# A graph-attention kernel's first stretch: index conversion moved to ScalarE, loads reordered, two blocks of work exchanged

## The chip, the cores and the metric

The kernel runs on one core of one Trainium2 chip. The metric is the device time of one execution in microseconds (us). Three runs of the kernel before gave 1695.93, 1697.75 and 1699.25 us; their median is 1697.75 us.

## The reference

The kernel computes one graph-attention layer with a residual and a layer norm. There are 6250 nodes of 96 features (4 heads of 24), and 200000 edges, each with a source and a destination node, sorted by destination.

```
q = (x[src] @ qW).reshape(e, 4, 24)
k = (x[dst] @ kW).reshape(e, 4, 24)
v = (x[dst] @ vW).reshape(e, 4, 24)
exp_s = exp(clip(einsum('ehd,ehd->eh', q, k), -10, 10))
norms = segment_sum(exp_s, src)[src]
w = exp_s / (norms + 1e-8)
res = segment_sum(w[:, :, None] * v, src).reshape(6250, 96)
out = layernorm(x + (x + res))
```

Here the edges' sources (`src`) are what the sums run over, and they are in no order; the destinations (`dst`) are sorted.

## The kernel before, in words

The program has four stretches: a first stretch that projects the nodes and makes all index tables (0 to about 133 us), a first phase that sorts the edges by source tile (`first_phase`, L434), a second phase that attends over the sorted edges (`second_phase`, L450), and the layer norm with the stores. The change touches the first stretch alone.

Each engine has its own program, and all its instructions run in the order in which they are written there; semaphores tie the engines together. In the first stretch two kinds of work are interleaved by hand.

**Projection of the nodes.** The 6250 nodes are 12 tiles of 512 nodes (`TI` = 12, t = 0 to 11) and a rest. For tile t, SyncE (SP) loads the rows (`rows_of_x`, L720) into a ring of three buffers. TensorE turns them (`turn_x`, L982, into one_c or one_d), ScalarE copies the turned tile to SBUF (`turned_x`, L843), and TensorE multiplies by the three weights (`project`, L991, one half into two_a and one into two_b). Then the float32 result is cut into three bfloat16 parts: `high` on ScalarE (L851), `rest_of` on VectorE (L1235: the projection less its high part), `mid` on ScalarE (L860), the low part on GpSimd (POOL, L607), and `keep_q` on ScalarE (L864). GpSimd also clears a tenth of `acc` (L611) behind each of the first ten. SP writes the parts to the table in HBM (L750) and issues four transfers that clear rows (`clear`, L713) in every step t. `project(t)` overwrites two_a and two_b, so it waits for `rest_of(t - 1)`.

**Index tables.** The source and destination of every edge are loaded as int32 in two arrays of 112 rows by 1792 (`edge_i`, `dest_i`; L726, L733, L736: three transfers each, 672, 105 and 4 KB). VectorE converts both to float32 (`edge_f`, L1249; `dest_f`, L1251). TensorE turns the sources in four groups (`sources`, L1008, into meta and sum_bank), VectorE copies each group out as int32 (L1274), and four VectorE instructions of 1568 elements split the node numbers into tile and place (L1277 to L1280, called the four bit operations below). The destinations follow in the steps t = 2 and 3 (`targets`, L1015, copied out by ScalarE at L880). From t = 4 on, seven pieces of a histogram are made (VectorE L1326, TensorE L1038, VectorE L1334), then prefix sums.

**Constants.** GpSimd fills its constant tiles at the start (L545 to L602). VectorE waits for them (`consts`) and derives twelve small constants from them (L1257 to L1269).

The order on the engines around the change: PE does `turn_x(0)`, waits for the weights, and then in every step `turn_x(t + 1)`, `project(t)`; `sources()` stands behind `project(1)`. ScalarE does `turned_x(0)`, `turned_x(1)`, and then per step `mid(t - 1)`, `keep_q(t - 2)`, `high(t)`, `turned_x(t + 2)`. VectorE does the conversion of the sources, `rest_of(0)`, the conversion of the destinations, `rest_of(1)`, the constants, the four copies of turned sources, the four bit operations, `rest_of(2)`, and then the destinations' part. SP issues x tile 0, both first pieces of the edges, the three weights, the four smaller pieces of the edges, x tiles 1 and 2, and then goes on by steps.

Of the kernel before, what the change touches and what calls it, by code (L numbers as in the profile page):

```python
# [16 lines left out]
ALU = mybir.AluOpType  # L17
ACT = mybir.ActivationFunctionType
# [13 lines left out]
COLS = 14  # L32
# [21 lines left out]
HI, LO = 7, 8  # L54
# [7 lines left out]
def gnn_program(nc, x, src, dst, wq, wk, wv, out):  # L62
# [57 lines left out]
    with ExitStack() as ctx:  # L120
# [3 lines left out]
        def sem(name):  # L124
            return ctx.enter_context(nc.semaphore(name))
# [209 lines left out]
        consts = sem("consts")  # L335
        later_consts = sem("later_consts")
        loads = sem("loads")
        edges_in = sem("edges_in")
        dve_step = sem("dve_step")
        edges_f = sem("edges_f")  # L340
        turned_src = sem("turned_src")
# [180 lines left out]
        def columns_of(held, n):  # L522
            return held[:, :, 4 * n:4 * n + turn_cols(n)].rearrange("p i k -> p k i")

        def turned_edges(n):
            return turn_in[n % 2][:, 0:turn_cols(n) * ITERS].rearrange("p (k i) -> p k i", k=turn_cols(n))
# [185 lines left out]
        def _(sp):  # L712
# [7 lines left out]
            def rows_of_x(t):  # L720
                sp.dma_start(x_in[:, t % XRING], x[t * TSLOT * P:(t + 1) * TSLOT * P, :].rearrange("(s p) d -> p s d", p=P)
                             ).then_inc(x_loaded[t % XRING], 16)

            rows_of_x(0)
            for flat, held in ((src, edge_i), (dst, dest_i)):
                sp.dma_start(held[0:EDGE_ROWS, :], flat[0:EDGE_ROWS * EIT].rearrange("(i e) -> i e", e=EIT)  # L726
                             ).then_inc(edges_in, 16)
            for n, w in enumerate((wk, wv, wq)):
                sp.dma_start(weights[0:D, n * D:(n + 1) * D], w).then_inc(loads, 16)

            sp.wait_ge(dve_step, 2)
            for flat, held in ((src, edge_i), (dst, dest_i)):
                sp.dma_start(held[EDGE_ROWS:ITERS - 1, :],  # L733
                             flat[EDGE_ROWS * EIT:(ITERS - 1) * EIT].rearrange("(i e) -> i e", e=EIT)
                             ).then_inc(edges_in, 16)
                sp.dma_start(held[ITERS - 1:ITERS, 0:EREST],  # L736
                             flat[(ITERS - 1) * EIT:E].rearrange("(i e) -> i e", i=1)).then_inc(edges_in, 16)
            for t in range(1, XRING):
                rows_of_x(t)
            for t in range(TI):  # L740
                if t + XRING <= TI:
# [100 lines left out]
        def _(act):  # L842
# [21 lines left out]
            def keep_q(t):  # L864
                act.wait_ge(low_made, t + 1)
                act.activation(q3[:, t * TSLOT:(t + 1) * TSLOT], parts3[:, t % 2, :, 2], ACT.Copy).then_inc(q_kept, 1)

            turned_x(0)
            turned_x(1)
            for t in range(TI + 1):  # L870
                if t >= 1:
                    mid(t - 1)
                if t >= 2:
                    keep_q(t - 2)
                if t < TI:
                    high(t)
                for n in TARGETS_AT.get(t, ()):

                    act.wait_ge(turned_dst, n + 1)
                    act.activation(columns_of(dcol_i, n), turned_edges(n), ACT.Copy).then_inc(kept_dst, 1)  # L880
                if t + 2 <= TI:
                    turned_x(t + 2)
# [95 lines left out]
        def _(pe):  # L978
# [91 lines left out]
            turn_x(0)  # L1070
            pe.wait_ge(loads, 48)
            for t in range(TI):
                turn_x(t + 1)
                project(t)
                if t == 1:
                    sources()
                if t in TARGETS_AT:
                    targets(TARGETS_AT[t])
                if t == BASES_AT:
                    bases()  # L1080
                for i in PIECES_AT.get(t, ()):
                    if i == 0:
                        pe.wait_ge(consts, NCONST)
                    piece(i)
                if t == 8:
                    totals()
                if t == 9:
                    starts()
                if t == 10:
                    steps()  # L1090
                if t == 11:
                    tiles_of_blocks()
# [131 lines left out]
        def _(dve):  # L1224
# [20 lines left out]
                                                last3[0:NREST, :, 0], ALU.subtract)  # L1245
                    ins.then_inc(rest_made, 1)

            dve.wait_ge(edges_in, 96)
            dve.tensor_copy(edge_f[0:ITERS], edge_i[0:ITERS]).then_inc(edges_f, 1)  # L1249
            rest_of(0)  # L1250
            dve.tensor_copy(dest_f[0:ITERS], dest_i[0:ITERS]).then_inc(edges_f, 1)  # L1251
            rest_of(1)

            dve.wait_ge(consts, NCONST)
            last = slice(P - 32, P)
# [11 lines left out]
            link(dve.tensor_scalar(tail_col, place_i[:, 1:2], float(P), float(P * FULL), ALU.mult, ALU.add))  # L1267
            link(dve.tensor_scalar(select_h, spread_h, next_col, None, ALU.is_equal))
            link(dve.scalar_tensor_tensor(select_h, spread_h, high_col, select_h, ALU.is_equal, ALU.subtract))  # L1269


            for n in range(4):
                dve.wait_ge(turned_src, n + 1)
                dve.tensor_copy(columns_of(col_i, n), turned_edges(n)).then_inc(kept_src, 1)  # L1274
            dve.wait_ge(kept_src, 4)
            bits = edge_i.rearrange("p (g c) -> p g c", c=COLS)[:, 0:NG]
            link(dve.tensor_scalar(bits, col_i, 7, LO - 1, ALU.logical_shift_right, ALU.bitwise_and))  # L1277
            link(dve.tensor_copy(src_lo, bits))
            link(dve.tensor_single_scalar(bits, col_i, 7, ALU.logical_shift_right))
            link(dve.tensor_copy(src_tile, bits))  # L1280
            rest_of(2)


# [370 lines left out]
```

## Time and profile before

| what | value |
|---|---|
| median of three runs | 1697.75 us |
| the profiled execution's own time | 1694.7 us |
| span of its trace | 1692.6 us |
| granted TensorE clock, mean over the span | 0.933 |
| PE busy | 1471.8 us (87%) |
| DVE busy | 1468.6 us (87%) |
| ACT busy | 1013.3 us (60%) |
| POOL busy | 1016.2 us (60%) |

PE is TensorE, PEld its weight loads, DVE VectorE, ACT ScalarE, POOL GpSimd, SP SyncE. The profile follows one execution. The own time is the span and about 2 us around it. The shares of busy time are means over four stretches that have different limits, so for a change in the first 133 us the stretch has to be looked at by itself. The granted clock is given as a share of 2.4 GHz: 1.00 is 2.4 GHz, 0.50 is 1.2 GHz.

### The profile page before, as it was taken

What the parts mean: (1) busy time and instruction counts of PE and PEld (TensorE: products, weight loads), DVE (VectorE), ACT (ScalarE), POOL (GpSimd) and SP (SyncE); (2) the same over time, 40 slices, a digit from 0 to 9 for tenths busy, and PEclk for the clock granted to TensorE, in tenths of its full rate; (3) what the DMA queues carried; (4) which work ended last, traced back from release to release, by engine and by line L of the source; (5) the groups of instructions that cost most, each with busy time, mean ns of one, the idle gap of its engine ahead of it and who ended that gap; (6) DMA issues with size and microseconds to landing.
All of it is one profiled execution on the core that took longest, in us unless ns stands there. A gap on an engine that the chain in (4) does not pass through costs nothing.

```text
span 1692.6 us, 56067 instructions
## 1 busy us (share of the span) xinstructions
PE 1471.8 (87%) x19964; PEld 1414.8 (84%) x19965; DVE 1468.6 (87%) x2980; ACT 1013.3 (60%) x1844; POOL 1016.2 (60%) x764
## 2 busy tenths in 40 slices
PE   4873988899888888898759999999999999999990
PEld 3652888888888888788759999999999999999990
DVE  6988999898898989989148999999999999999987
ACT  3341666566665666666536666666666666666654
POOL 6230777777777777767625555555555555555551
PEclk7565999999999999999979999999999999999995
DMA  5673899999999999999887777777777777777732
GB/s 166 225 273 132 310 373 357 351 334 360 345 364 344 352 351 350 367 318 371 328 297 258 243 242 241 244 246 246 241 244 241 243 245 246 244 241 241 244 113 57
DMA packets 159451, 465.03 MB, mean 275 GB/s; under 512 B 36994, under 2 KB 59266, under 8 KB 152244
## 3 DMA queue, kind: packets, MB, share of 16 engines
q1 hardware_dynamic: 123572, 301.16, 54.5%
q0 software_dynamic: 35840, 163.36, 24.1%
q8 instruction: 23, 0.38, 0.1%
q14 instruction: 16, 0.13, 0.0%
HBM read 271.21 MB, written 209.73 MB: 284 GB/s over the span
## 4 chain that ended last, share of the span: by engine, by line
PE 79%; DVE 9%; issue 7%; SPq 2%; DMA 2%; ACT 1%; POOL 0%; DVEq 0%; POOLq 0%; ACTq 0%
PE two_a L1133 14%; PE meta L1195 13%; PE sum_bank L1195 12%; PE two_b L1133 12%; PE two_a L1216 7%; PE two_b L1216 7%; PE one_c L1206 3%; PE one_d L1206 3%; PE meta L1151 2%; PE one_d L1162 2%; PE sum_bank L1115 1%; SPq L826 1%; DMA work<-kv_table 1%; DVE work L1472 1%; DVE acc L1618 1%
## 5 line engine op out<-in xcount | busy, mean ns | idle before, releaser
L699 POOL TENSOR_TENSOR work<-work 128x768 f32<-128x768 f32 x236 | 452.3, 1917 | 346.4 <-ACT work L941 346.4
L636 POOL DMA_INDIRECT sorted_rows<-work x448 | 501.1, 1118 | 209.6 <-issue 209.0
L1133 PE MATMUL two_a<-work 128*128 128x192 bf16 x2688 | 269.8, 252 | 80.1 <-issue 78.7
L1133 PEld LDWEIGHTS two_a<-work 128*128 128x128 f16 x2688 | 221.1, 100 | 100.8 <-issue 82.4
L904 ACT ACTIVATE work<-two_a 128x768 f32<-128x768 f32 x224 | 181.8, 811 | 179.8 <-PE two_a L1133 179.5
L1133 PE MATMUL two_b<-work 128*128 128x192 bf16 x2688 | 267.1, 251 | 0.0
L950 ACT ACTIVATE work<-work 128x1024 f32<-128x1024 bf16 x236 | 247.5, 1049 | 0.0
L1195 PE MATMUL meta<-work 128*128 128x100 f32 x1888 | 236.9, 279 | 0.9 <-DVE acc L1550 0.9
L1195 PE MATMUL sum_bank<-work 128*128 128x100 f32 x1888 | 235.2, 278 | 0.0
L1583 DVE TENSOR_REDUCE work<-work 128x32 f32<-128x768 f32 x236 | 224.9, 953 | 8.2
L1133 PEld LDWEIGHTS two_b<-work 128*128 128x128 f16 x2688 | 225.5, 100 | 6.7
L1195 PEld LDWEIGHTS meta<-work 128*128 128x128 f32 x1888 | 221.8, 193 | 1.0 <-issue 1.0
L1195 PEld LDWEIGHTS sum_bank<-work 128*128 128x128 f32 x1888 | 220.1, 192 | 0.0
L904 ACT ACTIVATE work<-two_b 128x768 f32<-128x768 f32 x224 | 181.9, 812 | 48.6 <-PE two_b L1133 48.2
L941 ACT ACTIVATE work<-work 128x32 f32<-128x32 f32 x236 | 54.1, 229 | 257.5 <-DVE work L1558 257.5
L1566 DVE TENSOR_TENSOR work<-work,node_row 128x1024 bf16<-128x1024 bf16 x236 | 161.9, 686 | 25.6 <-ACT work L934 25.6
L1216 PE MATMUL two_a<-q,work 128*128 x2832 | 141.9, 207 | 4.6 <-ACT work L947 4.6
L1216 PE MATMUL two_b<-q,work 128*128 x2832 | 140.4, 206 | 0.0
L1216 PEld LDWEIGHTS two_a<-q,work 128*128 128x128 bf16 x2832 | 130.3, 99 | 5.4 <-issue 5.2
L1574 DVE TENSOR_TENSOR work<-two_a,work 128x768 f32<-128x768 f32 x118 | 113.0, 958 | 23.6 <-PE two_a L1216 16.5
L1574 DVE TENSOR_TENSOR work<-two_b,work 128x768 f32<-128x768 f32 x118 | 113.0, 958 | 22.1 <-PE two_b L1216 22.0
L1216 PEld LDWEIGHTS two_b<-q,work 128*128 128x128 bf16 x2832 | 129.3, 98 | 0.0
(229 smaller groups left out, 2205.8 us busy)
## 6 DMA issues: line engine op xcount, KB each, us to landing
work<-sorted_rows SPq DMA_DIRECT2D x472, 392.0 KB, 3.5
work<-sorted_local SPq DMA_DIRECT2D x56, 1024.0 KB
sorted_rows<-pad_rows SPq DMA_DIRECT2D x49, 392.0 KB, 4.5
work<-kv_table SPq DMA_DIRECT2D x112, 144.0 KB
sorted_rows<-work POOLq DMA_INDIRECT x448
kv_table<-work SPq DMA_DIRECT2D x12, 576.0 KB, 3.4
work<-in_x SPq DMA_DIRECT2D x12, 192.0 KB, 3.8
sorted_local<-work SPq DMA_DIRECT2D x56, 8.0 KB
```

What stands on the lines that cost most here:

```text
L636: pool.indirect_dma_start(out=rows_dram, out_offset=bass.IndirectOffsetOnAxis(ap=place_now[:, p, u, b:b + 1], axis=0), in_=payload[:, p, u ...
L699: pool.tensor_tensor(now[:, :, 0:D].rearrange("p c (h f) -> p c h f", h=HEADS), blk[:, k, :, :, D:2 * D].rearrange("p m c (h f) -> p (m c) ...
L904: act.activation(payload[:, p, u, KPART * part:KPART * (part + 1), 0:2 * D].rearrange("p (b k) w -> p b k w", b=2), kv_ps[part % 2], ACT.C ...
L941: act.activation(msg[:, k % MSGS, :, D:AW], clipped[:, k], ACT.Exp).then_inc(exp_made[k % PSEM], 1)
L950: act.activation(hot_f[:, k % HOTF], hot[:, k % HOTS], ACT.Copy).then_inc(hotf_made[k % PSEM], 1)
L1133: mm = pe.matmul(to, picked[:, u % 2, k * P:(k + 1) * P], window[:, u, :, n, :], start=(n == 0), stop=(n == 2))
L1195: mm = pe.matmul(sums[k % 2][:, m, :], hot_f[:, k % HOTF, m * BLK + c, :], msg[:, k % MSGS, m * BLK + c, :], start=(c == 0), stop=(c == BL ...
L1206: mm = pe.transpose(turned[k % 2][:, c, :], hot[:, k % HOTS, c, :], ident_b[:])
L1216: mm = pe.matmul(q_ps[k % 2][:, m, c, :], hot_T[:, k % 2, m * BLK + c, :], q3[:, bass.ds(tile, 1), i, :].rearrange("p a d -> p (a d)"), st ...
L1566: dve.tensor_tensor(hot[:, k % HOTS].rearrange("p c (n i) -> p c n i", i=TWIN), tags[:, k].unsqueeze(2).to_broadcast([P, CH, P // TWIN, TW ...
L1574: dve.tensor_tensor(qk.rearrange("p (m c) d -> p m c d", m=PAIR), q_ps[k % 2], blk[:, k, :, :, 0:D], ALU.mult).then_inc(qk_made[k % PSEM], 1)
L1583: dve.tensor_reduce(score[:, k], qk.rearrange("p c (h f) -> p (c h) f", h=HEADS), AX.X, ALU.add).then_inc(score_made[k % PSEM], 1)
```

## The change

ScalarE converts both index arrays, through a new function `floats`, instead of VectorE. The semaphore `edges_in`, which counted all six transfers of the edges (96), is split into `sources_in` and `targets_in` (48 each). SP issues x tile 0, the weights, the sources, x tile 1, the destinations, x tile 2. TensorE does `project(0)` ahead of `turn_x(1)`. ScalarE does `high(0)`, the sources' conversion, `turned_x(1)`, the destinations' conversion, and goes on as before. On VectorE the copies of the turned sources and the four bit operations stand ahead of the constants.

```diff
-        edges_in = sem("edges_in")
+        sources_in = sem("sources_in")
+        targets_in = sem("targets_in")
...
+            def edges(flat, held, done):
+
+                sp.dma_start(held[EDGE_ROWS:ITERS - 1, :],
+                             flat[EDGE_ROWS * EIT:(ITERS - 1) * EIT].rearrange("(i e) -> i e", e=EIT)
+                             ).then_inc(done, 16)
+                sp.dma_start(held[ITERS - 1:ITERS, 0:EREST],
+                             flat[(ITERS - 1) * EIT:E].rearrange("(i e) -> i e", i=1)).then_inc(done, 16)
+
             rows_of_x(0)
-            for flat, held in ((src, edge_i), (dst, dest_i)):
-                sp.dma_start(held[0:EDGE_ROWS, :], flat[0:EDGE_ROWS * EIT].rearrange("(i e) -> i e", e=EIT)
-                             ).then_inc(edges_in, 16)
             for n, w in enumerate((wk, wv, wq)):
                 sp.dma_start(weights[0:D, n * D:(n + 1) * D], w).then_inc(loads, 16)
-
+            sp.dma_start(edge_i[0:EDGE_ROWS, :], src[0:EDGE_ROWS * EIT].rearrange("(i e) -> i e", e=EIT)
+                         ).then_inc(sources_in, 16)
             sp.wait_ge(dve_step, 2)
...
-            for t in range(1, XRING):
+            edges(src, edge_i, sources_in)
+            rows_of_x(1)
+            sp.dma_start(dest_i[0:EDGE_ROWS, :], dst[0:EDGE_ROWS * EIT].rearrange("(i e) -> i e", e=EIT)
+                         ).then_inc(targets_in, 16)
+            edges(dst, dest_i, targets_in)
+            for t in range(2, XRING):
                 rows_of_x(t)
...
+            def floats(held, ints, done):
+                act.wait_ge(done, 48)
+                act.activation(held[0:ITERS], ints[0:ITERS], ACT.Copy).then_inc(edges_f, 1)
+
             turned_x(0)
-            turned_x(1)
             for t in range(TI + 1):
...
                 if t < TI:
                     high(t)
+                if t == 0:
+                    act.wait_ge(dve_step, 2)
+                    floats(edge_f, edge_i, sources_in)
+                    turned_x(1)
+                    floats(dest_f, dest_i, targets_in)
...
             for t in range(TI):
-                turn_x(t + 1)
-                project(t)
+                if t == 0:
+                    project(t)
+                    turn_x(t + 1)
+                else:
+                    turn_x(t + 1)
+                    project(t)
...
-            dve.wait_ge(edges_in, 96)
-            dve.tensor_copy(edge_f[0:ITERS], edge_i[0:ITERS]).then_inc(edges_f, 1)
             rest_of(0)
-            dve.tensor_copy(dest_f[0:ITERS], dest_i[0:ITERS]).then_inc(edges_f, 1)
             rest_of(1)
+
+            for n in range(4):
+                dve.wait_ge(turned_src, n + 1)
+                dve.tensor_copy(columns_of(col_i, n), turned_edges(n)).then_inc(kept_src, 1)
...
             dve.wait_ge(consts, NCONST)
```

The instructions on ScalarE from its start, before the change (one_c and one_d hold a turned tile, two_a and two_b the halves of a projection):

```order
L849 ACTIVATE work<-one_c 96x512
L849 ACTIVATE work<-one_d 96x512
L857 ACTIVATE work<-two_a 128x6x96
L857 ACTIVATE work<-two_b 128x6x96
L849 ACTIVATE work<-one_c 96x512
L862 ACTIVATE work<-work 128x12x96
L857 ACTIVATE work<-two_a 128x6x96
L857 ACTIVATE work<-two_b 128x6x96
```

and with it:

```order
L855 ACTIVATE work<-one_c 96x512
L863 ACTIVATE work<-two_a 128x6x96
L863 ACTIVATE work<-two_b 128x6x96
L876 ACTIVATE work<-work 112x1792
L855 ACTIVATE work<-one_d 96x512
L876 ACTIVATE work<-work 112x1792
L855 ACTIVATE work<-one_c 96x512
L868 ACTIVATE work<-work 128x12x96
L863 ACTIVATE work<-two_a 128x6x96
L863 ACTIVATE work<-two_b 128x6x96
```

The two conversions (L876) stand ahead of everything that ScalarE does for tile 1 and later, the second of them behind the copy of turned tile 1.

VectorE from `rest_of(1)` to `rest_of(2)`, before the change (of the twelve constants the first and the last ones are shown, in two pieces):

```order
L1242 TENSOR_TENSOR work<-two_b,work 128x576
L1257 TENSOR_SCALAR work<-work 32x512
L1258 SCALAR_TENSOR_TENSOR work<-work 32x512
```

```order
L1268 TENSOR_SCALAR work<-work 128x1024
L1269 SCALAR_TENSOR_TENSOR work<-work 128x1024
L1274 CAST work<-meta 128x4x112
L1274 CAST work<-sum_bank 128x4x112
L1274 CAST work<-meta 128x4x112
L1274 CAST work<-sum_bank 128x2x112
L1277 TENSOR_SCALAR work<-work 128x1568
L1278 CAST work<-work 128x1568
L1279 TENSOR_SCALAR work<-work 128x1568
L1280 CAST cols_work<-work 128x1568
L1242 TENSOR_TENSOR work<-two_a,work 128x576
```

and with it:

```order
L1260 TENSOR_TENSOR work<-two_b,work 128x576
L1271 CAST work<-meta 128x4x112
L1271 CAST work<-sum_bank 128x4x112
L1271 CAST work<-meta 128x4x112
L1271 CAST work<-sum_bank 128x2x112
L1274 TENSOR_SCALAR work<-work 128x1568
L1275 CAST work<-work 128x1568
L1276 TENSOR_SCALAR work<-work 128x1568
L1277 CAST cols_work<-work 128x1568
L1282 TENSOR_SCALAR work<-work 32x512
L1283 SCALAR_TENSOR_TENSOR work<-work 32x512
```

The copies (L1271) and the bit operations (L1274 to L1277) now follow `rest_of(1)` at once, and the constants stand between them and `rest_of(2)`.

## Rows read from the trace of the kernel before

**Rows 1.** The page: share of the chain that ended last, by engine
```profile
PE 79%; DVE 9%; issue 7%; SPq 2%; DMA 2%; ACT 1%; POOL 0%; DVEq 0%; POOLq 0%; ACTq 0%
```

**Rows 2.** Windows: stretch, busy us of PE, PEld, DVE, ACT, POOL, clock, DMA, GB/s
```profile
0.00:12.20 12.20, 1.06 (x4) 0.65 (x5) 1.31 (x3) 1.88 (x2) 11.56 (x34) 1.00 0.92 187
12.20:21.00 8.80, 5.38 (x16) 3.86 (x16) 8.78 (x2) 2.37 (x4) 8.80 (x19) 1.00 0.60 208
21.00:70.50 49.50, 32.93 (x116) 25.23 (x117) 45.58 (x53) 21.07 (x27) 14.86 (x14) 0.60 0.55 197
70.50:101.00 30.50, 30.50 (x118) 27.00 (x118) 22.17 (x30) 11.36 (x15) 7.67 (x5) 0.58 0.65 229
101.00:132.90 31.90, 15.17 (x41) 8.62 (x38) 28.11 (x57) 14.81 (x19) 11.56 (x8) 0.58 0.77 285
```

**Rows 3.** Chain of waits in order of time: start us, us, what
```profile
5.31 6.81 DMA work<-in_dst
...
12.22 8.78 DVE work L1249
...
132.92 1.33 DVE work L1412
```

**Rows 4.** Timeline, 0 to 28 us: start us, us, engine, line, operation, [idle <-releaser]
```profile
4.48 0.59 ACT L849 ACTIVATE work<-one_c 96x512 f32<-96x512 f32 x1 [2.40 <-PE one_c L988]
...
5.60 1.49 SPq L721 DMA_DIRECT2D work<-in_x  x3
...
12.79 1.06 PE L988 MATMUL one_d<-ident_f,work 128*96 128x128 f32 x4 [8.35 <-DMA work<-in_x]
...
13.64 2.13 PE L997 MATMUL two_a<-work 96*128 96x288 f32 x4
...
17.73 0.65 ACT L857 ACTIVATE work<-two_b 128x576 bf16<-128x576 f32 x1 [1.27 <-PE two_b L997]
...
21.15 0.10 POOL L602 MEMSET start_i<- 1x9 int32 x1
...
21.80 2.26 PE L997 MATMUL two_a<-work 96*128 96x288 f32 x4 [3.62 <-DVE work L1242]
22.24 1.08 DVE L1251 CAST work<-work 112x1792 f32<-112x1792 int32 x1
...
25.77 0.95 PE L1004 MATMUL meta<-ident_f,work 112*128 112x112 f32 x4
...
26.69 0.76 DVE L1242 TENSOR_TENSOR work<-two_b,work 128x576 f32<-128x576 f32 x1 [1.16 <-ACT work L857]
```

**Rows 5.** Timeline, 27 to 43 us
```profile
27.48 0.35 DVE L1257 TENSOR_SCALAR work<-work 32x512 bf16<-32x512 bf16 x1
...
32.14 0.92 DVE L1274 CAST work<-meta 128x448 int32<-128x448 f32 x1
...
35.51 0.98 DVE L1277 TENSOR_SCALAR work<-work 128x1568 int32<-128x1568 int32 x1
...
37.14 2.59 POOL L607 TENSOR_TENSOR work<-work 128x1152 bf16<-128x1152 f32 x1 [10.72 <-ACT work L862]
37.53 3.48 DVE L1279 TENSOR_SCALAR work<-work 128x1568 int32<-128x1568 int32 x1
...
39.67 0.52 POOL L611 MEMSET acc<- 128x500 f32 x1
...
42.06 0.76 DVE L1242 TENSOR_TENSOR work<-two_a,work 128x576 f32<-128x576 f32 x1
```

**Rows 6.** Groups of ScalarE by form, 0 to 140 us: busy us, mean ns
```profile
L862 ACT ACTIVATE work<-work 128x1152 bf16<-128x1152 f32 x12 | 13.9, 1157 | 11.9 <-DVE work L1242 11.9
...
L880 ACT ACTIVATE work<-meta 128x448 int32<-128x448 f32 x2 | 1.9, 944 | 0.0
```

**Rows 7.** By line, one instruction's ns min/median/max: the projection; a histogram piece
```profile
L997 PE MATMUL two_b<-work x48: 406/684/687, 15.6 to 124.2; 96*128 96x288 f32 x48
...
L1038 PE MATMUL meta<-work x42: 409/413/419, 60.4 to 88.2; 128*112 128x128 f16 x42
```

More of the change, by code:

```diff
@@ L722, in rows_of_x @@
                              ).then_inc(x_loaded[t % XRING], 16)
+            def edges(flat, held, done):
[4 more added lines that the diff above has]
+                             flat[(ITERS - 1) * EIT:E].rearrange("(i e) -> i e", i=1)).then_inc(done, 16)
             rows_of_x(0)
-            for flat, held in ((src, edge_i), (dst, dest_i)):
-                sp.dma_start(held[0:EDGE_ROWS, :], flat[0:EDGE_ROWS * EIT].rearrange("(i e) -> i e", e=EIT)
-                             ).then_inc(edges_in, 16)
             for n, w in enumerate((wk, wv, wq)):
                 sp.dma_start(weights[0:D, n * D:(n + 1) * D], w).then_inc(loads, 16)
+            sp.dma_start(edge_i[0:EDGE_ROWS, :], src[0:EDGE_ROWS * EIT].rearrange("(i e) -> i e", e=EIT)
+                         ).then_inc(sources_in, 16)
             sp.wait_ge(dve_step, 2)
[L732 to L737, printed above, removed]
-            for t in range(1, XRING):
+            edges(src, edge_i, sources_in)
[4 more added lines that the diff above has]
+            for t in range(2, XRING):
                 rows_of_x(t)
@@ L1246, in rest_of @@
                     ins.then_inc(rest_made, 1)
-            dve.wait_ge(edges_in, 96)
-            dve.tensor_copy(edge_f[0:ITERS], edge_i[0:ITERS]).then_inc(edges_f, 1)
             rest_of(0)
-            dve.tensor_copy(dest_f[0:ITERS], dest_i[0:ITERS]).then_inc(edges_f, 1)
             rest_of(1)
+            for n in range(4):
+                dve.wait_ge(turned_src, n + 1)
+                dve.tensor_copy(columns_of(col_i, n), turned_edges(n)).then_inc(kept_src, 1)
+            dve.wait_ge(kept_src, 4)
+            bits = edge_i.rearrange("p (g c) -> p g c", c=COLS)[:, 0:NG]
+            link(dve.tensor_scalar(bits, col_i, 7, LO - 1, ALU.logical_shift_right, ALU.bitwise_and))
+            link(dve.tensor_copy(src_lo, bits))
+            link(dve.tensor_single_scalar(bits, col_i, 7, ALU.logical_shift_right))
+            link(dve.tensor_copy(src_tile, bits))
             dve.wait_ge(consts, NCONST)
@@ L1269, in _ @@
             link(dve.scalar_tensor_tensor(select_h, spread_h, high_col, select_h, ALU.is_equal, ALU.subtract))
[L1272 to L1280, printed above, removed]
             rest_of(2)
```

## The prediction

> **What bounds the kernel now.** The page's split of the chain that ended last says PE 79% and VectorE 9% [rows 1], but that is a mean over the whole span. The change ends where the first phase begins, at 132.92 us [rows 3], so I read the first stretch alone. The windows come first [rows 2]. From 0 to 12.2 us VectorE does 1.31 us of work, then it is full: 8.78 of 8.80 us, then 45.58 of 49.50 us. From 70.5 to 101 us TensorE is full (30.50 of 30.50), and after that VectorE again (28.11 of 31.90). The chain in order of time says what stands at the start [rows 3]: a transfer of the destinations that lands at 12.12, and behind it one instruction of VectorE, the conversion of the sources (L1249), 8.78 us long.
>
> The timeline shows why that is odd [rows 4]. The same instruction on the destinations (L1251, same shape) takes 1.08 us at 22.24. The long one begins at 12.22 and ends at 21.00; GpSimd is busy for 8.80 of the 8.80 us from 12.2 to 21.0 [rows 2], and its last constant ends at 21.25 [rows 4]. So 7.7 of the 8.78 us are VectorE waiting for GpSimd. Everything hangs behind it: `rest_of(0)`, and TensorE's `project(1)`, which starts at 21.80 after 3.62 us idle, released by VectorE.
>
> **The change part by part.**
>
> *Project 0 ahead of turn 1.* ScalarE has turned tile 0 at 5.07 [rows 4]. Before, `project(0)` starts at 13.64, behind x tile 1 (TensorE idle 8.35 us on that transfer). Now it needs only the weights. Their landing is not shown; they follow x tile 0 directly, so at least 5.1, and at most 3.0 + 6.8 = 9.8 us (they are issued by about 3.0, at 0.5 us per issue as the three of 1.49 us at 5.60 [rows 4], and the slowest transfer shown took 6.81 us, behind a full queue [rows 3]). I take 5.4, near the lower end, since x tile 0 alone is ahead. From its start, `high(0)` ends 4.74 us later (18.38 - 13.64), so at 10.1, and `rest_of(0)`, two instructions of 0.75, ends at about 10.9. VectorE then is free for ten microseconds in which it was waiting.
>
> *Loads.* Before, x tile 1 was issued from 5.60 and TensorE started on it at 12.79 [rows 4]. In the new order the same bytes stand ahead of x tile 2 as did before: all edges, the weights, tiles 0 and 1. Tile 2 is 192 KB behind tile 1; at the 208 to 229 GB/s of the windows [rows 2] that is 0.8 to 0.9 us, so tile 2 lands at about 13.5. The destinations land between 12.1 and 12.8, plus what x tile 1 ahead of them adds: about 13.0. The sources land earlier, at about 8: they and what is ahead of them are 1.1 MB of the 1.9 MB that had landed at 12.12, counted from 2. If the queue were no faster for them they land at 12.1; then ScalarE's two conversions run back to back from 12.1 to 15.5, which costs about 0.5.
>
> *Conversion on ScalarE.* No row shows it. Nearest below: 1152 elements in 1157 ns (L862), which for 1792 gives 1.8 us. Nearest above: ScalarE writing int32, 448 elements in 944 ns (L880) [rows 6], 2.1 ns each, 3.8 us. L880 reads PSUM and writes with a stride; L862 goes from SBUF to SBUF in rows like the conversion, so I take 1.8. ScalarE then has: sources' conversion 10.1 to 11.9; `turned_x(1)` (0.59) to 12.5; destinations' conversion 13.0 to 14.8; `turned_x(2)` to 15.4; `mid(0)` (1.16) to 16.6.
>
> *Tile 1.* TensorE turns tile 2 at 13.5 (0.85 to the projection, as 12.79 to 13.64), and `project(1)` starts at 14.35, against 21.80: 7.45 us earlier. `high(1)` needs its first half at 16.6; ScalarE is free at 16.6. That is tight, but nothing is lost. `rest_of(1)` ends 5.65 us after the start of `project(1)` (27.45 - 21.80), so at 20.0. `sources()` begins 3.97 us after `project(1)` (25.77 - 21.80) and the first group is turned at about 19.3, so VectorE goes from `rest_of(1)` straight to the copies.
>
> *Sources ahead of constants.* Moving the constants costs and saves VectorE nothing by itself: 27.48 to 32.11, 4.6 us [rows 5], only stand elsewhere. TensorE and ScalarE get the sources 4.6 us earlier, but `project(3)` waits for `rest_of(2)`, which still stands behind both blocks. What the move changes is which of VectorE's work meets GpSimd. The four copies take 3.35 us (32.14 to 35.5), now 20.0 to 23.4; they read PSUM, and so does L1242, which takes 0.76 here and there [rows 4, 5]. GpSimd's constants still end at 21.25; then it has L607 and L611 for tile 0, together about 2.9 us (37.14 to 40.19 [rows 5], less a short wait at the start), to 24.1. The first bit operation waits for them from 23.4: 0.7 us lost. L607 for tile 1 follows at about 25.1, when the first bit operation ends; with L611 it ends at 28.0. Before, L1279 (37.53 to 41.01, 3.48 for what takes 0.98) waited so, ending 0.8 behind L611 [rows 5]. Now the second one does: it ends at 28.8, the fourth at 30.8, the constants at 35.5, and there `rest_of(2)` starts, against 42.06 [rows 5]: **6.6 us earlier** (7.45, less 0.7 and some tenths of worse overlap).
>
> The Trainium skill ("SBUF — State Buffer", "Who interferes with whom") says that VectorE's two-port instructions and GpSimd exclude each other, the later one blocked until the instruction that holds the ports has finished. By that alone the second bit operation would slip in between L607 and L611, and the gain would be 0.5 us more, about 7.1, within the forecast's own bounds. The row speaks against that rule in its simple form: the conversion waited through some twenty instructions of GpSimd, not one, and L1279 went on only after L611.
>
> *The rest of the stretch.* From `rest_of(2)` on, nothing is changed, and GpSimd's L607 stands where it stood relative to VectorE. VectorE's part to 70.5 and TensorE's to 101 shift as they are: the histogram's matmuls take 409 to 419 ns at any time of the stretch, whatever the clock, and the projections 406 or 684 ns by the clock [rows 7]. The first stretch's granted clock is 0.60 and 0.58 [rows 2], so it changes within it. If the fast times fall otherwise, a projection of eight matmuls gains or loses about 2 us (8 x 0.28), of which one or two stand on the path. I take nothing and put 2 us each way in the range. SP's waits (`low_made` for tile 0) stay pinned near 24 by GpSimd's constants, as before; x tile 4 is issued behind them and is wanted at about 28, so it hides. Were it late, `turn_x(4)` would hold `project(3)`, which waits until 35.5 anyway.
>
> **Sum.** 1694.7 - 6.6 = 1688.1 us for an execution like the profiled one. The median of the runs stands 3.05 us above that execution, so the median forecast is 1697.75 - 6.6 = **1691.2 us**.
>
> **The rivals.**
>
> *A, VectorE is kept out for longer* (chance 0.15). The row for L1249 shows that it can be starved through back-to-back GpSimd work. If L607 of tile 1 follows the first L611 at once, none of the four bit operations gets in until 28.0, and they end at 31.8: a gain of 5.6, 1692.2 us.
>
> *B, more than forecast* (0.15). Tile 2 lands earlier, or an L607 that now stretches VectorE (1.0 to 2.5 us each, as L1279) meets a PSUM read instead; or the clock is kinder. One such piece on top: 9 us, 1688.8.
>
> *C, no gain that can be told* (0.14). The 6.6 us are given back before 132.9, in the stretch where TensorE is the bound, or the loads order doesn't help since all transfers share the same 16 engines and land together at 12 to 15. If x tile 2 lands at 18, `project(1)` starts at 18.85 and the gain is 2.9; with 2 us lost to the clock it is 1: 1696.8. For it: 0.92 of the engines' time in the first 12.2 us [rows 2]. Against it: the queue had landed tile 1 by 12.79.
>
> *D, slower: ScalarE's queue becomes the bound* (0.04). Behind the destinations' conversion stand `turned_x(2)`, `mid(0)` and `high(1)`, and VectorE waits for `high(1)`. With a conversion of c us, `rest_of(1)` ends at 10.1 + c + 0.6 + c + 0.6 + 1.2 + 1.3 + 0.8 = 14.6 + 2c. That reaches the 27.45 of before at c = 6.4. If ScalarE took for it the 8.78 us that VectorE did, it would end at 32.2: 4.7 us later than before, 1702.5. Against: L857 takes 0.65 us at 17.73, in the middle of GpSimd's constants [rows 4], so ScalarE isn't stretched by them, and 6.4 us is 3.5 times the nearest row's rate.
>
> That the change doesn't do what it says is excluded by the order of the instructions: both conversions are on ScalarE and project 0 is ahead.
>
> **How the numbers follow.** The forecast itself (5.9 to 8 us) has 0.52. The executions shown lie 3.3 us apart, so about 0.2%, or 3.4 us, is what a measurement can tell from no change. Faster by more than that: forecast, A and B, less a tail, 0.80. Within: C and that tail, 0.16. Slower: D, 0.04. The range reaches down to a gain of 11.5 (B at 9, 2 by the clock, 0.5 in the ports) and up to a gain of 2 (C's better half): 1686.2 to 1695.8.
>
> **What would show it right or wrong.** Right: project 0 starts at 5 to 6 us; each conversion on ScalarE takes about 1.8 us; `project(1)` at 14 to 15; `rest_of(1)` ends at about 20; one or two bit operations are stretched, ending at 31; the first instruction of the first phase (L1412 before) starts at about 126.3. Wrong: `project(1)` later than 17, a conversion over 3 us, all four bit operations behind 28, or VectorE at 35 us as forecast but the first phase no earlier than 131.

## The result, and the profile after

The changed kernel takes 1708.02 us (median of six runs, 1705.72 to 1708.33), the kernel before 1695.74 (six runs, 1693.76 to 1699.25). The ratio is 1.0067, with a 95% interval from 1.0054 to 1.008: slower by 0.7%. The forecast was 1691.2 us, and the range ended at 1695.8.

The profiled execution took 1708.07 us, its span is 1706.0 us and its mean granted clock 0.945. Where the difference of 13.4 us to the own time of before lies:

| part | before, us | after, us | difference |
|---|---|---|---|
| first stretch, to the first phase's first instruction | 132.92 | 124.92 | -8.0 |
| first phase, to the first one-hot of the second phase | 725.5 | 726.8 | +1.3 |
| second phase, from the first one-hot to the last | 778.9 | 798.9 | +20.0 |
| from there to the end of the span | 55.3 | 55.3 | 0 |

The first stretch gained more than forecast. The second phase, over 700 us behind everything that the change touches, lost over twice that. The one-hot is the VectorE instruction that compares a row of node numbers with a pair's sources. By line, its durations are minimum, median and maximum in ns; before:

```profile
L1566 DVE TENSOR_TENSOR work<-work,node_row x236: 682/684/694, 858.4 to 1637.3; 128x1024 bf16<-128x1024 bf16 x118
```

After:

```profile
L1580 DVE TENSOR_TENSOR work<-work,node_row x236: 683/685/1994, 851.8 to 1650.7; 128x1024 bf16<-128x1024 bf16 x118
```

The median is the same, the longest is three times as long. 27 of the 236 are about 1.99 us: the seventeenth and every eighth after it. Each turn of the loop handles eight pairs, so it is always the same place of the turn. A turn of the loop takes 27.14 us where it took 26.37, and 27 x 0.77 = 20.8 us covers the 20.0 of the table.

The timeline at that place before the change (start, us, engine, line, operation):

```profile
1205.00 0.17 DVE L1558 TENSOR_SCALAR work<-work 128x32 f32<-128x32 f32 x1
...
1205.23 0.26 DVE L1550 TENSOR_TENSOR acc<-acc,meta 128x100 f32 x1
1205.44 0.69 DVE L1566 TENSOR_TENSOR work<-work,node_row 128x1024 bf16<-128x1024 bf16 x1
1205.51 1.97 POOL L699 TENSOR_TENSOR work<-work 128x768 f32<-128x768 f32 x1 [1.36 <-ACT work L941]
```

And after, at the same place:

```profile
1206.11 0.17 DVE L1572 TENSOR_SCALAR work<-work 128x32 f32<-128x32 f32 x1
1206.46 0.26 DVE L1564 TENSOR_TENSOR acc<-acc,meta 128x100 f32 x1 [0.17 <-issue]
1206.63 1.49 POOL L700 TENSOR_TENSOR work<-work 128x768 f32<-128x768 f32 x1 [1.37 <-ACT work L955]
1206.67 1.99 DVE L1580 TENSOR_TENSOR work<-work,node_row 128x1024 bf16<-128x1024 bf16 x1
```

Before, the one-hot starts 0.07 us ahead of GpSimd's multiply, runs at its usual 0.69 us, and the multiply is stretched to 1.97. After, the small sum ahead of it (`acc<-acc,meta`) starts 0.35 us behind the instruction before it instead of 0.23. So the one-hot starts 0.04 us behind GpSimd's multiply. The multiply now takes 1.49 us, and the one-hot ends 0.54 us behind it. The late start is put down to "issue": VectorE waited for nothing that the profile shows. Among VectorE's waits from 900 to 1650 us (the same columns as below) this line stands after the change, and none like it before:

```profile
DVE acc L1564 <- issue: 4.9, 27, 0.4
```

At the other seven places the one-hot leads by 0.07 to 0.19 us, within 0.01 us the same in both traces. The Trainium skill ("SBUF — State Buffer", "Who interferes with whom") says that, where the two engines contend, whichever issues first holds the shared ports for its whole instruction. The trace agrees: a difference of 0.11 us in a start turns 0.69 us into 1.99.

TensorE then waits for VectorE's next sum. Its waits from 900 to 1650 us (engine, tile, line, what for: us in total, times, longest) after:

```profile
PE sum_bank L1213 <- DVE acc L1564: 16.2, 27, 0.6
```

and before:

```profile
PE meta L1195 <- DVE acc L1550: 0.9, 1, 0.9
```

The page's groups after say the same (busy us, mean ns, idle before and releaser):

```profile
L1213 PE MATMUL sum_bank<-work 128*128 128x100 f32 x1888 | 235.3, 278 | 16.2 <-DVE acc L1564 16.2
...
L1580 DVE TENSOR_TENSOR work<-work,node_row 128x1024 bf16<-128x1024 bf16 x236 | 196.9, 834 | 27.3 <-ACT work L948 27.3
```

The page's chain has moved the same way, from [rows 1] to

```profile
PE 67%; DVE 14%; issue 12%; DMA 2%; SPq 2%; DVEq 2%; ACT 1%; POOL 0%; POOLq 0%; ACTq 0%
```

The first stretch itself, in the windows of [rows 2] and in their columns:

```profile
0.00:12.20 12.20, 6.33 (x16) 3.82 (x17) 2.83 (x5) 5.08 (x6) 11.56 (x34) 1.00 0.85 178
12.20:21.00 8.80, 5.81 (x20) 4.35 (x20) 1.37 (x2) 4.80 (x6) 8.80 (x22) 1.00 0.73 220
21.00:70.50 49.50, 32.95 (x131) 27.36 (x132) 46.95 (x56) 18.58 (x24) 13.88 (x10) 0.73 0.68 242
70.50:101.00 30.50, 25.25 (x97) 20.87 (x95) 24.01 (x36) 15.78 (x20) 12.37 (x8) 0.72 0.64 226
```

TensorE projects from 5.4 us on. In the second window VectorE was busy for 8.78 us, about 7.7 of them waiting inside one conversion; now it is 1.37. The clock between 21 and 101 us is 0.73 and 0.72, where it was 0.60 and 0.58 (from there to the first phase it is 0.50, where it was 0.58). The timeline, in place of [rows 4] and [rows 5]:

```profile
5.43 2.26 PE L1011 MATMUL two_a<-work 96*128 96x288 f32 x4 [0.77 <-ACT work L855]
...
10.19 1.69 ACT L876 ACTIVATE work<-work 112x1792 f32<-112x1792 int32 x1
...
14.03 1.70 ACT L876 ACTIVATE work<-work 112x1792 f32<-112x1792 int32 x1 [1.67 <-DMA work<-in_dst]
...
14.77 1.06 PE L1002 MATMUL one_c<-ident_f,work 128*96 128x128 f32 x4 [3.94 <-DMA work<-in_x]
...
15.62 2.13 PE L1011 MATMUL two_a<-work 96*128 96x288 f32 x4
...
20.28 0.10 POOL L603 MEMSET start_i<- 1x9 int32 x1
...
20.39 0.76 DVE L1260 TENSOR_TENSOR work<-two_b,work 128x576 f32<-128x576 f32 x1 [1.16 <-ACT work L863]
...
26.05 3.49 DVE L1276 TENSOR_SCALAR work<-work 128x1568 int32<-128x1568 int32 x1
...
35.25 0.76 DVE L1260 TENSOR_TENSOR work<-two_a,work 128x576 f32<-128x576 f32 x1
```

It reads much as forecast: project 0 at 5.43, conversions of 1.69 and 1.70 us, one stretched bit operation (3.49 us), `rest_of(2)` at 35.25 against 42.06 [rows 5].

### The profile page after: what moved, and what is told of

Read it like the earlier page. It is cut to its first block, busy times and chain, and to the rows that moved or that the text cites. A ratio compares the mean times of both kernels' runs of the same rounds, so it can differ in the third digit from the quotient of the medians.

```text
span 1706.0 us, 56068 instructions
## 1 busy us (share of the span) xinstructions
PE 1470.1 (86%) x19964; PEld 1410.9 (83%) x19965; DVE 1491.3 (87%) x2978; ACT 1016.2 (60%) x1846; POOL 1006.9 (59%) x764
## 4 chain that ended last, share of the span: by engine, by line
PE 67%; DVE 14%; issue 12%; DMA 2%; SPq 2%; DVEq 2%; ACT 1%; POOL 0%; POOLq 0%; ACTq 0%
PE two_a L1151 13%; PE two_b L1151 12%; PE sum_bank L1213 10%; PE meta L1213 10%; PE two_a L1234 5%; PE two_b L1234 5%; DVE work L1588 3%; PE meta L1169 2%; PE one_d L1224 2%; PE one_c L1224 2%; PE one_d L1180 2%; DVE acc L1564 1%; DMA work<-kv_table 1%; DVEq L507 1%; PE sum_bank L1133 1%
## 5 line engine op out<-in xcount | busy, mean ns | idle before, releaser
L700 POOL TENSOR_TENSOR work<-work 128x768 f32<-128x768 f32 x236 | 438.6, 1859 | 378.9 <-ACT work L955 378.9
L637 POOL DMA_INDIRECT sorted_rows<-work x448 | 506.2, 1130 | 207.1 <-issue 207.1
L1151 PE MATMUL two_a<-work 128*128 128x192 bf16 x2688 | 266.2, 250 | 87.5 <-issue 84.8
L1580 DVE TENSOR_TENSOR work<-work,node_row 128x1024 bf16<-128x1024 bf16 x236 | 196.9, 834 | 27.3 <-ACT work L948 27.3
```

Of the source, the lines that this page charges most:

```text
L637: pool.indirect_dma_start(out=rows_dram, out_offset=bass.IndirectOffsetOnAxis(ap=place_now[:, p, u, b:b + 1], axis=0), in_=payload[:, p, u ...
L700: pool.tensor_tensor(now[:, :, 0:D].rearrange("p c (h f) -> p c h f", h=HEADS), blk[:, k, :, :, D:2 * D].rearrange("p m c (h f) -> p (m c) ...
L1151: mm = pe.matmul(to, picked[:, u % 2, k * P:(k + 1) * P], window[:, u, :, n, :], start=(n == 0), stop=(n == 2))
L1580: dve.tensor_tensor(hot[:, k % HOTS].rearrange("p c (n i) -> p c n i", i=TWIN), tags[:, k].unsqueeze(2).to_broadcast([P, CH, P // TWIN, TW ...
```

## Experiments: where the second phase's loss comes from

Nothing of the change stands in the second phase. What differs there is where its code lies: VectorE's program has 831 instructions instead of 833 and its second loop begins at instruction 561 instead of 563; ScalarE's has 485 instead of 482. TensorE's, GpSimd's and SP's are as long as before. The theory was that the loop's place in VectorE's program (P) makes the small sum late. The rivals were the time or the state in which the second phase is entered (T) and ScalarE's length (S). The first four share 23 runs of the kernel before (median 1694.31). In e1 to e3, waits that have long been fulfilled are added, which do nothing but lengthen a program (a loop of five waits adds two instructions, one of three adds one); in e4 one wait sets an order.

**e1_after_vec2.** VectorE's length of before, with the change otherwise whole.

```diff
+            for _ in range(5):
+                dve.wait_ge(dve_step, 2)
             rest_of(0)
```

> The changed kernel with two instructions that only wait (for something long done) added on VectorE in the first stretch, where it is idle. Its loops then stand as far from the start of VectorE's program as in the kernel before; nothing else differs. Theory P (the place of VectorE's second loop in its program makes one instruction per loop turn 0.12 us late, so that GpSimd's multiply starts 0.04 us ahead of VectorE's one-hot instead of 0.07 behind it): no one-hot is longer than 0.70 us, the loop turns take 26.37 us instead of 27.14, the run takes 1708 - 21 = about 1687 us. Theory T (the change in the first stretch moves the time at which the second phase is entered, and the engines settle in another rhythm): the same 27.14 us and 1708 us, since nothing in time is moved by more than 0.2 us.

Measured: 1689.12 us (six runs), ratio 0.997 (0.9953 to 0.9988). The first phase starts at 125.10, a turn takes 26.37 us, and the one-hots by line are:

```profile
L1582 DVE TENSOR_TENSOR work<-work,node_row x236: 682/684/694, 849.5 to 1627.1; 128x1024 bf16<-128x1024 bf16 x118
```

Two more instructions on VectorE, none of which does anything, take the loss away. The first one-hot comes at 849.5 us, 2.3 us earlier than with the change, so this run alone leaves T a little room; all traces together leave it none. The sum is late (0.34 to 0.35 us behind the instruction before it, not 0.23) in the five whose VectorE program has 831 instructions (the change, e4, e6, e7, e8), with a first one-hot at 851.3 to 856.4 us, and in none of the other nine, with a first one-hot at 848.3 to 861.9.

**e2_before_vec2.** The same two instructions on the kernel before (835).

```diff
+            for _ in range(5):
+                dve.wait_ge(dve_step, 2)
             dve.wait_ge(edges_in, 96)
```

> The kernel before with two such instructions added on VectorE, ahead of its wait for the edges. Theory P with a pattern that repeats every four instructions: adding two is the same as removing two, the loop turns take 27.14 us and the run about 1717 us. Theory P with a longer repeat, or with a place that only the two missing ones reach: 1696 us. Theory T: 1696 us.

Measured: 1694.93 us (ten runs), ratio 1.0005 (0.9993 to 1.0017); first phase at 133.01, turns of 26.37 us. Length as such costs nothing; that 835 would be a bad place too is not borne out.

**e3_before_sca3.** ScalarE's length of the change on the kernel before.

```diff
+            for _ in range(6):
+                act.wait_ge(dve_step, 2)
             turned_x(0)
```

> The kernel before with three such instructions added on ScalarE, as the change adds three to its program. Rival S (it is ScalarE's place, or its lead over GpSimd, that counts): slow loop turns of 27.14 us, about 1717 us. Theories P and T: 1696 us.

Measured: 1694.02 us (ten runs), ratio 0.9999 (0.9985 to 1.0013); first phase at 131.62, turns of 26.37 us. That rules S out.

**e4_fix.** The changed kernel, its lengths as they were, where GpSimd's multiply waits for the pair's late sum. In `weigh`:

```diff
                         pair_done(pool, exp_made, k, back, at_j)
+                        if late := lagged(s, LA, j, drain):
+                            pair_done(pool, acc_made, *late, at_j)
                         now = msg[:, k % MSGS]
```

> The changed kernel, VectorE's program untouched; in the second phase GpSimd's multiply also waits for VectorE's second sum of the same step, the instruction just ahead of the one-hot. If the order of the two starts is the cause of the long one-hots, whatever makes VectorE late, GpSimd can no longer start first: no one-hot over 0.75 us, turns of 26.4 to 26.5 us, 1687 to 1690 us. If the long one-hots have another cause (the wait of VectorE is not for GpSimd): 27.1 us turns and 1708 us or more.

Measured: 1689.26 us (six runs), ratio 0.9964 (0.9945 to 0.9983); first phase at 125.69, turns of 26.37 us. The timeline at the place of the loss:

```profile
1015.49 0.17 DVE L1574 TENSOR_SCALAR work<-work 128x32 f32<-128x32 f32 x1
...
1015.83 0.26 DVE L1566 TENSOR_TENSOR acc<-acc,meta 128x100 f32 x1 [0.17 <-issue]
1016.04 0.69 DVE L1582 TENSOR_TENSOR work<-work,node_row 128x1024 bf16<-128x1024 bf16 x1
1016.24 1.84 POOL L702 TENSOR_TENSOR work<-work 128x768 f32<-128x768 f32 x1 [1.60 <-DVE acc L1566]
```

The sum is still late (0.34 us, "issue"), but GpSimd now waits for it, and the one-hot leads by 0.20 us. So the lateness alone costs nothing: the order of two starts is what costs 0.77 us a turn.

**e8_before_floats_sca.** The kernel before with one part of the change, the conversions on ScalarE, which makes VectorE 831 long.

```diff
             turned_x(0)
+            act.wait_ge(dve_step, 2)
+            act.wait_ge(edges_in, 96)
+            for held, ints in ((edge_f, edge_i), (dest_f, dest_i)):
+                act.activation(held[0:ITERS], ints[0:ITERS], ACT.Copy).then_inc(edges_f, 1)
...
-            dve.wait_ge(edges_in, 96)
-            dve.tensor_copy(edge_f[0:ITERS], edge_i[0:ITERS]).then_inc(edges_f, 1)
             rest_of(0)
-            dve.tensor_copy(dest_f[0:ITERS], dest_i[0:ITERS]).then_inc(edges_f, 1)
```

> The kernel before with one part of the change alone: both conversions on ScalarE, between turned_x(0) and turned_x(1). It takes two instructions from VectorE's program as the change does, at other times. Theory P: VectorE's second sum is 0.11 us late once per turn, turns take 27.14 us, the run about 1711 us (first phase at about 129.2 us, 3.7 earlier; second phase 21 us longer). Theory T' (it takes the change's own timing of the second phase's entry as well): 26.37 us turns and about 1690 us.

Measured: 1712.41 us (two runs), ratio 1.0095 (1.0066 to 1.0124). By line, the one-hots, and the first phase's first instruction in the timeline:

```profile
L1567 DVE TENSOR_TENSOR work<-work,node_row x236: 682/684/1995, 856.4 to 1655.7; 128x1024 bf16<-128x1024 bf16 x118
...
129.10 1.33 DVE L1413 TENSOR_TENSOR work<-cols_work,tile_row 128x1400 f16<-128x1400 f16 x1
```

As theory P said, 3.8 us are won in the first stretch, and the loss is back in full, in a kernel with nothing else of the change in it.

**e10_after_vec1, e11_after_vec8, e12_after_vec16.** The changed kernel, VectorE's program longer by 1, 8 and 16 instructions, by e1's loop with 3 turns for the first and 33 for the last.

> The changed kernel with one instruction added on VectorE instead of the two of e1_after_vec2. Theory P with one bad place: turns of 26.37 us and about 1687 us. If the parity or a wider region counts: 27.14 us, 1708 us.

> The same with eight instructions added on VectorE. A pattern that repeats every 8 instructions (or 2 or 4, which e1 and e2 exclude): 27.14 us turns and 1708 us. Otherwise 26.37 us and 1687 us.

> The same with sixteen. A pattern that repeats every 16 instructions: 27.14 us turns and 1708 us. Otherwise 26.37 us and 1687 us.

One execution each, 1688.34, 1692.02 and 1685.31 us; the kernel before had 1697.21 (median of nine runs) beside them. The first phase starts at 125.57, 125.32 and 126.44, and the turns are 26.37 us in all three (in e11 a single one-hot near the end takes 1.81 us). So the late sum doesn't come back at any of these distances, which leaves a pattern that repeats every 32 instructions or more untested. Of the lengths that ran, 831, 832, 833, 835, 839 and 847, only 831 has it.

## Experiments: what each part is worth in the first stretch

e5, e6 and e7 have e4's wait in them, so that the second phase is out of the account; e9 is the kernel before with one edit. All are read by the start of the first phase (125.69 us in e4). The total of one execution is no measure here: the first phase alone took 723.4 to 729.1 us in these traces. The start of the first phase varies too. Six kernels do the same work in the first stretch, but for some waits that are long fulfilled (the change, e1, e4, e10, e11, e12), and start the first phase at 124.92 to 126.44 us, one trace each; the kernel before, e2 and e3 start it at 132.92, 133.01 and 131.62. A difference of less than 1.5 us between two traces is therefore not told from none.

**e5_floats_on_vec.** The conversions go back to VectorE, everything else stays.

```diff
                 if t == 0:
-                    act.wait_ge(dve_step, 2)
-                    floats(edge_f, edge_i, sources_in)
                     turned_x(1)
-                    floats(dest_f, dest_i, targets_in)
...
             rest_of(0)
+            for held, ints, done in ((edge_f, edge_i, sources_in), (dest_f, dest_i, targets_in)):
+                dve.wait_ge(done, 48)
+                dve.tensor_copy(held[0:ITERS], ints[0:ITERS]).then_inc(edges_f, 1)
             rest_of(1)
```

> The changed kernel with GpSimd's extra wait of e4_fix, and both conversions back on VectorE, between rest_of(0) and rest_of(1); the new order of loads and of TensorE stays. Theory (VectorE's conversion is kept out by GpSimd's constants): the sources' conversion starts near 11 and ends near 21, rest_of(1) ends near 23.7 instead of 21.1, the first phase starts at about 128.3 us instead of 125.7 (e4_fix). Rival (the gain of the first stretch comes from the loads and from project 0, not from the conversion): a conversion of about 1.1 us that is done by 13, first phase at 125 to 126.

Measured: 1690.01 us (five runs), ratio 0.9949 (0.9932 to 0.9966); the first phase starts at 126.14, 0.45 us later than in e4, which is inside that spread. The timeline:

```profile
11.08 1.56 DVE L1268 CAST work<-work 112x1792 f32<-112x1792 int32 x1
...
11.63 1.04 POOL L584 IOTA node_col<- 128x1 f32 x1
...
13.52 1.15 DVE L1268 CAST work<-work 112x1792 f32<-112x1792 int32 x1 [0.88 <-DMA work<-in_dst]
```

My expectation was wrong, and the rival's was near. On VectorE, and in the midst of GpSimd's constants, the conversion takes 1.56 us and not 8.78: it starts 0.55 us ahead of a one-column iota of GpSimd, which takes 1.04 us in its place (0.14 in the kernel before, at 11.64). That VectorE starts the conversion at 11.08 and not at 12.22 [rows 3] matters more than which engine does it. e5 keeps the new orders of loads and projections, and nearly all of the gain; that ScalarE does the conversions isn't shown to be worth anything, in this start or in the runs' ratio (0.9949 here, 0.9964 in e4, with intervals that overlap).

**e9_small_later.** The kernel before, with that iota alone moved behind `tile_row`, so that it comes later and a waiting conversion meets it.

```diff
-                    (node_col[:], [[0, 1]], 0, 1), (node_row[:], [[1, P], [0, HC]], 0, 0),
+                    (node_row[:], [[1, P], [0, HC]], 0, 0),
                     (node1_row[:], [[1, P]], 1, 0), (tile_row[:], [[1, NB], [0, HC]], 0, 0),
+                    (node_col[:], [[0, 1]], 0, 1),
```

> The kernel before with one of GpSimd's constants, the one-column node_col, filled three places later, behind tile_row; nothing else differs. VectorE's conversion of the sources asks at 12.2 us, as before. Theory G (VectorE gets in only where GpSimd comes to an instruction so short that it leaves a gap): it gets in there, near 13.9, takes about 1 us and ends near 15 instead of 21.0; project 1 and everything behind it starts up to 3.5 us earlier and the first phase at 129 to 130 us instead of 132.9; 1691 us. Rival (VectorE is kept out until GpSimd's list is done): 8.8 us, ending at 21.0, 132.9 us.

Measured: 1694.24 us (eight runs), ratio 0.9987 (0.9971 to 1.0003), by which the total can't be told from no change. The timeline:

```profile
12.00 2.96 DVE L1250 CAST work<-work 112x1792 f32<-112x1792 int32 x1 [9.50 <-DMA work<-in_dst]
...
13.97 1.03 POOL L584 IOTA node_col<- 128x1 f32 x1
```

The conversion ends at 14.96 where it ended at 21.00, and the first phase starts at 128.93, against 132.92: half of the change's first-stretch gain, by the place of one constant. The rival, that VectorE is kept out until GpSimd's list is done, is ruled out. In the kernel before, the conversion waits through some twenty instructions of GpSimd and gets in only near the end of the list, beside the iota that is stretched to 1.07 us:

```profile
15.46 0.12 POOL L586 MEMSET ones_h<- 128x8 f16 x1
...
19.94 0.10 POOL L597 MEMSET tile_i<- 1x14 int32 x1
20.00 1.07 POOL L598 IOTA tile_i<- 1x49 int32 x1
```

Theory G, that a very short instruction is what lets it in, fits these three places (the one-column iota in e5 and e9, which takes 0.14 us when nothing stretches it, and the memset of 0.10 here), but it isn't shown as a rule: the 0.12 us memset at 15.46 is as short and did not let it in. And in e9 the second conversion waited through one instruction of GpSimd alone and got in beside a memset of 0.20 us:

```profile
18.59 1.60 DVE L1252 CAST work<-work 112x1792 f32<-112x1792 int32 x1
...
19.05 0.20 POOL L594 MEMSET work<- 128x128 f16 x1
```

What decides where VectorE gets in stays open.

**e6_consts_first.** The constants again ahead of the copies and bit operations.

```diff
             rest_of(1)
-            for n in range(4):
...
-            link(dve.tensor_copy(src_tile, bits))
             dve.wait_ge(consts, NCONST)
...
+            for n in range(4):
...
+            link(dve.tensor_copy(src_tile, bits))
             rest_of(2)
```

> The changed kernel with GpSimd's extra wait, and the constants back ahead of the copies of the turned sources on VectorE. My step said that this order alone moves nothing: first phase at 125.7 us, give or take 0.7. Rival (the sources' early copies let TensorE and ScalarE run ahead, and that is worth time): 127 us or later.

Measured: 1690.89 us (eight runs), ratio 0.9975 (0.9962 to 0.9989). The timeline:

```profile
21.01 2.29 DVE L1274 TENSOR_SCALAR work<-work 32x512 bf16<-32x512 bf16 x1
...
33.00 3.50 DVE L1294 TENSOR_SCALAR work<-work 128x1568 int32<-128x1568 int32 x1
...
127.75 1.32 DVE L1428 TENSOR_TENSOR work<-cols_work,tile_row 128x1400 f16<-128x1400 f16 x1
```

The first phase starts 2.06 us later than in e4, outside the 125.7 give or take 0.7 that I expected. The first constant, 0.35 us in [rows 5], takes 2.29: it falls under GpSimd's low part of tile 0, where the PSUM copies stood. A bit operation is still stretched, and `rest_of(2)` starts at 37.54. The rival's time came true, but 1.94 us of it are this one instruction.

**e7_turn_first.** TensorE turns tile 1 ahead of project 0 again.

```diff
-                if t == 0:
-                    project(t)
-                    turn_x(t + 1)
-                else:
-                    turn_x(t + 1)
-                    project(t)
+                turn_x(t + 1)
+                project(t)
```

> The changed kernel with GpSimd's extra wait, and TensorE's turn of tile 1 back ahead of project 0. project 0 then waits for x tile 1 (9.7 us), ScalarE's first conversion and turned_x(1) stand behind high(0), project 1 starts at about 17.6 instead of 15.6 and the first phase at about 127.7 us. Rival (this exchange is hidden behind the landing of x tile 2): 125.7 us.

Measured: 1691.46 us (seven runs), ratio 0.9979 (0.9961 to 0.9997). Project 0 starts at 11.01, project 1 at 17.86, and the first phase at 127.86, 2.17 us later than in e4 and close to the 127.7 expected. Like e6's 2.06 this is outside the spread, on one trace each.

## Why the prediction was wrong

**The step that failed** is the sum itself, by way of *The rest of the stretch*: "From `rest_of(2)` on, nothing is changed". I carried that through the first phase and the second, "1694.7 - 6.6", as if everything behind the first stretch moved as a whole, so the second phase stands in the sum with nothing, and no row was read for that. It measured +20.0 us. The instructions there are the same. What did change is VectorE's length ahead of them, which is in the order of the instructions for whoever counts them: two fewer. The runs put the +20 us on that, from three sides: e1 (length restored), e8 (length changed with one part of the change alone), e4 (order set by a wait). Why 831 instructions make the sum late they don't show. In the second phase of the kernel before two starts stood 0.07 us apart, with the later instruction stretched to 1.97 us. Rival D, the slower one, had another mechanism (ScalarE's queue) and didn't come about: ScalarE's conversions took 1.69 us, and 6.4 was its condition.

**The first stretch, point by point.** 8.0 us won between the two profiled executions, 6.6 forecast. By the spread of the other traces (131.62 to 133.01 before, 124.92 to 126.44 after) the gain is 5.2 to 8.1, so the two agree. With the second phase's loss taken away, the medians of whole runs fall by 5.2 us (e1) and 5.1 us (e4); 6.6 lies inside both intervals.

- *Project 0*: 5.43 against 5.4. `high(0)`'s second half is released at 10.3 against 10.1. Right.
- *Conversion on ScalarE*: 1.69 and 1.70 against 1.8. Right, but the reason for its worth was wrong: with the new order of loads and projections VectorE would have done it in 1.56 and 1.15 us (e5), and the 0.45 us between e5 and e4 lie inside the spread of such traces.
- *Loads*: the destinations let ScalarE go on at 14.03 (13.0 forecast), and x tile 2 reached TensorE at 14.77 (13.5). More than a microsecond late, so project 1 at 15.62 against 14.35.
- *GpSimd's constants* end at 20.38, not 21.25: the iota that took 1.07 us (shown under e9) takes 0.17 now that no conversion pushes into it. So tile 0's part on GpSimd was done by 23.2, not 24.1.
- *Sources ahead of constants*: the forecast gave the order no worth of its own ("costs and saves VectorE nothing by itself"), though it said that the order decides which of VectorE's work meets GpSimd. e6 puts 2.06 us on it, by that meeting.
- *Bit operations*: they ended at 30.56 against 30.8, but not as told. `rest_of(1)` ended at 21.15 and not at 20.0, the first bit operation didn't wait the 0.7 us, and the third one was stretched by 2.5 us, not the second.
- *`rest_of(2)`* at 35.25 against 35.5. The number is right by luck: the loads' delay and the waits and copies that came out shorter cancel.
- *From there to the first phase* another 1.2 us were won, less than the spread of these starts. The clock between 21 and 101 us was 0.73 and 0.72 instead of 0.60 and 0.58, behind it 0.50 instead of 0.58; whatever it gave lay inside the 2 us that I allowed. One reading of mine is loose here: "406 or 684 ns by the clock" doesn't hold at the start. Project 0 at 13.64 takes the slow time (2.13 us for four matmuls) in a window whose clock reads 1.00 [rows 2, 4], and so does the one at 15.62 now.

The sign that I named for being wrong (the first phase no earlier than 131) would have called this change a success. None of my signs lay behind the first stretch.

A version that beats both kernels is e4: the change with the order of the two starts set by a wait, 0.9964 (0.9945 to 0.9983) of the kernel before. e5, without the move to ScalarE, is as good, 0.9949 (0.9932 to 0.9966). e1, 0.997 (0.9953 to 0.9988), does as well, but by luck of place.

## What to carry to other kernels

In a steady loop that VectorE and GpSimd share, list the starts of each pair of instructions that collide, and by how much the right one leads. A lead of 0.07 us can hold for as long as nothing moves, and then cost its price in every turn; where the order matters, set it by a semaphore, which cost nothing here. And forecast a change to a straight piece of code with a look at the tightest place of every loop behind it, since a shift by two instructions on one engine was worth more than all that the edit did on purpose.

## What the runs showed of the hardware that I had not expected

- One VectorE instruction started 0.11 us later, in each of 27 turns, because the program ahead of it was two instructions shorter. Why is open. The instruction queues in the page's part 3 are the same in both traces, 23 packets with 0.38 MB in all and 16 with 0.13 MB, so no extra fetch shows there. From 950 to 1630 us of the trace after, where 25 of the 27 long one-hots lie, not one instruction packet stands among the transfers. The Trainium skill ("Runtime: NRT & Kernel Launch", "Instruction fetch mechanics") tells of instructions fetched in blocks of 256. No run here shows that this is the cause: 847 (16 more) did not bring the lateness back, and a shift by a whole block was not tried.
- VectorE's conversion can wait through many instructions of GpSimd, not one: 8.78 us in the kernel before, 2.96 in e9 and 1.56 in e5, for the same 112x1792 elements that take 1.08 at 22.24 [rows 4]. Moving a one-column iota moved the place where it got in.
- ScalarE was not held up by any of this: its conversion took 1.69 us at 10.19 with GpSimd busy throughout, and the same 1.69 in e7 at 15.64 and 17.71.
